# Both layers' rank rows in one result operand, results in the split x's memory, stores issued by ScalarE, SyncE's gathers spread around the x loads

## The reference

```python
def cond(x, A, B, ids):
    Bx = jnp.einsum('bni,bri->bnr', x, B[ids])
    return jnp.einsum('bnr,bor->bno', Bx, A[ids])
def L1_ffn(x, W, b, A, Bm, Wr):
    base_out = jnp.einsum('bsi,oi->bso', x, W) + b
    gates = softmax(jnp.einsum('bsi,ei->bse', x, Wr))
    proj_r = jnp.einsum('bsi,eri->bser', x, A)
    lora_out = jnp.einsum('bser,eor->bseo', proj_r, Bm)
    return base_out + jnp.einsum('bse,bseo->bso', gates * 2.0, lora_out)
x = x + L0_ffn(cond(x, L0_cond_A, L0_cond_B, itok_B_3_7), ...)
x = x + L1_ffn(cond(x, L1_cond_A, L1_cond_B, itok_B_4_50), ...)
```

## Time and profile before

| what | value |
|---|---|
| three runs, median (lowest to highest) | 353.43 us (350.32 to 354.69) |
| the profiled execution: its time / its span | 353.02 us / 351.0 us |
| TensorE matmuls busy | 326.0 us (93%), 2112 instructions |
| VectorE, ScalarE, GpSimd busy | 246.0 (70%), 149.8 (43%), 89.9 us (26%) |
| moved by DMA | 56.17 MB, mean 160 GB/s |

### The profile page before, as it was taken

One profiled execution on the slowest core, in us unless ns is written; L12 is line 12 of the kernel. 1 busy time (PEld: TensorE's weight loads), 2 busy tenths in 40 slices (PEclk: granted clock), 3 DMA queues, 4 the chain that ended last, 5 costly groups with the idle time before them and its releaser, 6 DMA issues.

```text
span 351.0 us, 6577 instructions
## 1 busy us (share of the span) xinstructions
PE 326.0 (93%) x2112; PEld 304.6 (87%) x2112; DVE 246.0 (70%) x496; ACT 149.8 (43%) x317; POOL 89.9 (26%) x61
## 2 busy tenths in 40 slices
PE   6998747889999999999999999999999999999975
PEld 5777647879999899989999999999999999999864
DVE  5925993797586867697668767775878586855554
ACT  5856833663065405550456036613562166203210
POOL 0014620184015500550046003620262026300000
PEclk9999898969999999999999999999999999999989
DMA  6889526611782078405950586048803780140005
GB/s 276 327 278 326 181 92 203 219 58 51 250 269 92 17 228 287 132 2 166 302 189 0 143 289 225 0 120 268 266 5 98 245 296 18 49 190 2 0 23 218
DMA packets 31525, 56.17 MB, mean 160 GB/s; under 512 B 3793, under 2 KB 21074, under 8 KB 31506
## 3 DMA queue, kind: packets, MB, share of 16 engines
q1 hardware_dynamic: 31506, 55.94, 47.9%
HBM read 39.15 MB, written 16.78 MB: 159 GB/s over the span
## 4 chain that ended last, share of the span: by engine, by line
PE 53%; issue 12%; DMA 10%; DVE 9%; POOL 6%; SPq 5%; ACT 4%; POOLq 0%; ACTq 0%; DVEq 0%
PE ps_d L316 12%; PE ps_d L318 12%; PE ps_d L317 12%; POOL xs_lo L917 5%; DMA xraw<-w 4%; DMA out<-xraw 3%; PE ps_h L323 3%; PE ps_p L316 2%; DVE k_lo L684 2%; PE ps_p L317 2%; PE ps_p L318 2%; PE ps_t L447 2%; DMA abraw<-ab_tab 2%; SPq L233 2%; SPq L235 2%
## 5 line engine op out<-in xcount | busy, mean ns | idle before, releaser
L917 POOL TENSOR_TENSOR xs_lo<-xraw,xs_hi 128x512 fp32r<-128x512 f32 x48 | 67.8, 1423 | 195.4 <-ACT xs_hi L520 195.3
L316 PE MATMUL ps_d<-w1s_hi,a1s_hi 128*128 128x384 f32 (+1 forms) x216 | 72.7, 337 | 1.8 <-DVE w1s_lo L684 1.8
L318 PE MATMUL ps_d<-w1s_hi,a1s_lo 128*128 128x384 f32 (+1 forms) x216 | 70.2, 325 | 0.0
L317 PE MATMUL ps_d<-w1s_lo,a1s_hi 128*128 128x384 f32 (+1 forms) x216 | 70.2, 325 | 0.0
L903 DVE SCALAR_TENSOR_TENSOR xraw<-ps_d,bsum,xraw 128x512 f32<-128x512 f32 x62 | 46.3, 750 | 27.5 <-PE ps_d L318 27.5
L520 ACT ACTIVATE xs_hi<-xraw 128x512 fp32r<-128x512 f32 x64 | 38.4, 624 | 17.6 <-DMA xraw<-x_in 11.1
L316 PEld LDWEIGHTS ps_d<-w1s_hi,a1s_hi 128*128 128x128 f32 x216 | 41.1, 190 | 3.9 <-DVE w1s_lo L684 3.8
L316 PE MATMUL ps_p<-xs_hi,bst_hi 128*128 128x256 f32 x128 | 39.4, 307 | 3.4 <-POOL xs_lo L917 2.5
L317 PEld LDWEIGHTS ps_d<-w1s_lo,a1s_hi 128*128 128x128 f32 x216 | 41.1, 190 | 0.0
L318 PEld LDWEIGHTS ps_d<-w1s_hi,a1s_lo 128*128 128x128 f32 x216 | 41.0, 190 | 0.0
L317 PE MATMUL ps_p<-xs_lo,bst_hi 128*128 128x256 f32 x128 | 37.8, 295 | 0.0
(11 more groups left out here) (156 smaller groups left out, 691.8 us busy)
## 6 DMA issues: line engine op xcount, KB each, us to landing
xraw<-x_in SPq DMA_DIRECT2D x32, 512.0 KB, 5.0
out<-xraw SPq DMA_DIRECT2D x32, 512.0 KB, 3.6
xraw<-w SPq DMA_DIRECT2D x16, 512.0 KB, 6.5
abraw<-ab_tab SPq DMA_DIRECT2D x64, 128.0 KB, 2.1
b0raw<-b_tab SPq DMA_DIRECT2D x64, 64.0 KB, 1.9
b0raw<-a SPq DMA_DIRECT2D x1, 512.0 KB, 3.7
lp<-exp SPq DMA_DIRECT2D x4, 69.0 KB, 7.5
cm<-exp_in SPq DMA_DIRECT2D x1, 144.0 KB, 5.3
```

The lines of the kernel that those rows point to most:

```text
L316: pe.matmul(acc, lh, rh, start=first, stop=False, skip_group_check=True)
L317: pe.matmul(acc, lh, rl, start=False, stop=False, skip_group_check=True)
L318: return pe.matmul(acc, ll, rh, start=False, stop=final, skip_group_check=True)
L917: return pool.tensor_tensor(dst, whole, high.bitcast(F32), ALU.subtract)
```

## The change

- **Result operand.** `res` [128, half, high/low, 1024] holds 64 rank rows of layer 1 and 64 rank rows of layer 0, the latter picked for the four sequences of a half. `from_layers(m)` takes it against the masked coefficients `cf` themselves (six matmuls of 256 columns). The experts' rows of both layers stand alone in `ew`, each twice in its 128 rows, against `ce`, whose rows hold the high and low parts of the coefficients: two matmuls of 512 columns.
- **Picking.** `m0` is stored to a DRAM table `m0_tab` ahead of the steps, and GpSimd fetches in each step the layer-0 rows of its eight sequences: `pick_m0`, eight DMAs of 16 rows x 2048 values (128 KB), after the last store of the step before has landed.
- **Expert part of the layer-1 coefficients.** `hle` x `ce`, two matmuls of 512 columns in place of six of 256; its splits have an instruction less.
- **Results** go to `done`, which lies over `xs` (the split x, used up by then), so that x loads wait for `d_out` only; ScalarE issues the stores at the end of its step; whoever writes `xs` again waits for `stored`.
- **SyncE's order.** Four sequences' gathers, x load 0, two sequences' gathers, x load 1, two sequences' gathers, x loads 2 and 3.
- **Start.** `hsb` and `lp` become one tile `misc`, which also receives layer 0's expert weights; it is zeroed after these are used (L773 of the changed kernel), and `init_done` moves to that memset. The experts' rows are loaded twice (ten small DMAs for five). In the last step, all five early result tiles start after `route(1)`.

```diff
+        xs_at = nc.sbuf_base
         xs = split("xs", [P, KT, HALF])
+
+        done_ = nc.alloc_sbuf_tensor_at("done", [P, KT * TOK], F32, offset=xs_at)
...
-        m1x = split("m1x", [P, 2, D])
+        res = sb("res", [P, 2, 2, D], F32R)
         k1 = split("k1", [P, TOK])
-        k2 = split("k2", [P, TOK])
-        c0s = split("c0s", [P, TOK])
+        cf = [sb(f"cf{i}", [P, 2, TOK], F32R) for i in range(2)]
+        ce = sb("ce", [P, TOK], F32R)
...
+                if k == 3:
+                    sp.wait_ge(m0_lo, len(WIDE_PARTS))
+                    sp.dma_start(m0_tab[:].rearrange("a r h n -> (a r) h n"), res[:, 0, :, :].bitcast(F32)
+                                 ).then_inc(m0_kept, 16)
                 if k == 6:
                     sp.wait_ge(w1_lo, 4)
-                    for e, n in enumerate(experts):
-                        r0 = E0ROWS[0].start + e * ER
-                        sp.dma_start(rows_raw[r0:r0 + ER, :],
-                                     exp0_rows[bass.ds(n, 1)].rearrange("a r o -> (a r) o")
-                                     ).then_inc(rows_in, 16)
-                    sp.dma_start(rows_raw[E1ROWS[0], :], exp1_rows).then_inc(rows_in, 16)
+                    for rows0, rows1 in (EHIGH, ELOW):
+                        for e, n in enumerate(experts):
+                            r0 = rows0.start + e * ER
+                            sp.dma_start(rows_raw[r0:r0 + ER, :],
+                                         exp0_rows[bass.ds(n, 1)].rearrange("a r o -> (a r) o")
+                                         ).then_inc(rows_in, 16)
+                        sp.dma_start(rows_raw[rows1, :], exp1_rows).then_inc(rows_in, 16)
...
-                    gather(picks, range(GROUP))
-                for i in range(CH):
-                    sp.wait_ge(d_out, KT * g + KC * (i + 1))
-                    sp.dma_start(out[bass.ds(g, 1), :, KC * i:KC * (i + 1), :]
-                                 .rearrange("a p k t -> p (a k) t"),
-                                 xraw[par][:, KC * i:KC * (i + 1), :]).then_inc(stored[i], 16)
-                    if ahead and i > 0:
-                        sp.wait_ge(stored[i - 1], 16 * g + 16)
-                        load_x(g + 2, par, i - 1)
-                if ahead:
-                    sp.wait_ge(stored[CH - 1], 16 * g + 16)
-                    load_x(g + 2, par, CH - 1)
+                    gather(picks, range(HSEQ))
+                    for i in range(CH):
+                        sp.wait_ge(d_out, KT * g + KC * (i + 1))
+                        load_x(g + 2, par, i)
+                        if i < 2:
+                            gather(picks, range(HSEQ + 2 * i, HSEQ + 2 * i + 2))
             steps(sp, body, 3)
...
-                product(ps_s[:], part(hts, ALL, ALL), part(k1, ALL, ALL), True, False)
-
-                pe.wait_ge(l_lo, 4 * g + 2)
-                for half in range(2):
-                    cols = slice(half * HALF, (half + 1) * HALF)
-                    mm = product(ps_s[:, cols], part(hls, ALL, half, ALL), part(k2, ALL, cols), False, True)
-                mm.then_inc(q_done, 1)
+                product(ps_s[:], hts, part(k1, ALL, ALL), True, False)
+
+                pe.wait_ge(l_lo, 2 * g + 1)
+                pe.matmul(ps_s[:], hle[:, 0, :], ce[:], start=False, stop=False, skip_group_check=True)
+                pe.matmul(ps_s[:], hle[:, 1, :], ce[:], start=False, stop=True, skip_group_check=True
+                          ).then_inc(q_done, 1)
...
-                def from_layer0(m):
-                    product(banks[m % len(banks)][:], part(m0s, ALL, slice(m * P, (m + 1) * P)), part(k1, ALL, ALL),
-                            True, False)
+                def from_layers(m):
+
+                    pe.wait_ge(m1_lo, 6 * g + (2 if m < 3 else 6))
+                    for half in range(2):
+                        cols = slice(half * HALF, (half + 1) * HALF)
+                        product(banks[m % len(banks)][:, cols],
+                                (res[:, half, 0, m * P:(m + 1) * P], res[:, half, 1, m * P:(m + 1) * P]),
+                                part(coefs, ALL, cols), half == 0, False)
...
-                    start_results((0, 1, 3))
+                    pe.wait_ge(m0_picked, 16 * GROUP * (g + 1))
                 else:
                     project(g + 1, 0)
                 pe.wait_ge(f1_lo, 2 * g + 2)
-                route(1, k2, f1s)
+                route(1, coefs, f1s)
+                pe.wait_ge(m0_picked, 16 * GROUP * (g + 1))
                 if last:
-                    start_results((4, 2))
+                    start_results((0, 1, 3, 4, 2))
...
-                        mm = product(banks[m % len(banks)][:, cols], part(m1x, ALL, half, slice(m * P, (m + 1) * P)),
-                                     part(k2, ALL, cols), False, True)
+                        from_layers(m)
+                    for w in (ew_hi, ew_lo):
+                        mm = pe.matmul(banks[m % len(banks)][:], w[:, m * P:(m + 1) * P], ce[:], start=False,
+                                       stop=w is ew_lo, skip_group_check=True)
...
+                    if half == 0:
+                        after_step(act, stored[i // KC], stored_by(g))
...
+                for i in range(CH):
+                    act.wait_ge(d_out, KT * g + KC * (i + 1))
+                    act.dma_start(out[bass.ds(g, 1), :, KC * i:KC * (i + 1), :]
+                                  .rearrange("a p k t -> p (a k t)"), done[i]).then_inc(stored[i], 16)
...
-            for t in (*hls, f1s, *k2):
+            for t in (hle, f1s, ce):
                 dve.memset(t[:].bitcast(F32), 0.0)
+            dve.memset(ew_lo[HR_:P, :].bitcast(F32), 0.0)
             dve.memset(hr[:, :, :, HC - 1:HC].bitcast(F32), 0.0)
-            dve.memset(hsb[:, 1, :], 0.0).then_inc(init_done, 1)
...
+            dve.tensor_copy(cb[:, 2, :], exp0_routerb).then_inc(small_lo, 1)
+            dve.wait_ge(small_lo, 3)
+            dve.memset(misc[:, P:], 0.0).then_inc(init_done, 1)
...
+                    if last and m % KC == 0:
+                        dve.wait_ge(stored[m // KC], 16 * g)
                     dve.wait_ge(d_done, KT * g + m + 1)
-                    dve.scalar_tensor_tensor(out=xraw[par][:, m, :], in0=banks[m % len(banks)][:],
+                    dve.scalar_tensor_tensor(out=done[m // KC][:, m % KC * TOK:(m % KC + 1) * TOK],
+                                             in0=banks[m % len(banks)][:],
...
+            def pick_m0(g):
+
+                layer0 = nc.values_load_multi_w_load_instructions(
+                    ids[0:1, bass.ds(g * GROUP, GROUP)], (mybir.EngineType.Pool,), min_val=0,
+                    max_val=ADAPT0 - 1)[1]
+                after_step(pool, d_done, KT * g)
+                after_step(pool, stored[CH - 1], 16 * g)
+                for b, n0 in enumerate(layer0):
+                    half = b // HSEQ
+                    r0 = L0ROWS[half].start + (b % HSEQ) * RANK
+                    pool.dma_start(res[r0:r0 + RANK, half, :, :],
+                                   m0_tab[bass.ds(n0, 1)].rearrange("a r h n -> (a r) h n")).then_inc(m0_picked, 16)
+
             split_x(0, 0, 0, range(CH))
             split_x(0, 0, 1, (0, 2))
             split_a(0)
+            pool.wait_ge(ids_in, 16)
+            pool.wait_ge(m0_kept, 16)
+            pick_m0(0)
             pool.wait_ge(w1_hi, POOL_CHUNK + 1)
             low(w1s[1][:, POOL_CHUNK, 0:D], w1raw[POOL_CHUNK], w1s[0][:, POOL_CHUNK, 0:D]).then_inc(w1_lo_pool, 1)
             def body(g, par, last):
+                if not (isinstance(g, int) and g == 0):
+                    pick_m0(g)
                 if not last:
```

139 lines of the change are left out of this document (69 added, 70 removed).

## The result

The changed kernel takes 399.1 us (median of 4 runs, 397.22 to 402.89) where the kernel before takes 353.4: a ratio of 1.132, 95% interval 1.121 to 1.143. It is 13% slower; 351 had been forecast, in a range that ends at 366. The profiled execution took 397.2 us, its span is 394.3.

A forecast was written before the change was run, and what follows sets the result against it. TensorE was taken to bound the steps, busy 35.89 of 36.20 us. 353.0 + 12.3 (start) - 1.5 - 2.1 - 1.0 (step 0) - 12.8 (steps) - 1.2 (last step) + 4.2 (waits) = 350.9, about 351; range 343 to 366.

The forecast's parts named there:

- the gathers, ahead of two x loads, at 5.5 to 7, I take 6.4: Loop steps: gathered rows land 6.4 us after the step's first ps_h matmul, so split_b ends at 8.6.
- rival 2: Loop steps: gathers queue against stores packet by packet, landing at about 8.6; 364 us or more; chance 0.13.
- 0.7 us a step: Loop steps: net new TensorE wait from late gathers and picks together, six times, +4.2 us.
- no slack: Before the transposes: today l_done at 216.67 meets turn() at 216.72; net wait put at 0 to 1.5 us a step.
- -8.6: Six loop steps: 12.8 us gained by fewer matmuls, 4.2 us lost to new waits.
- a step without waits: Loop steps: 34.1 us each, plus waits that name l_done or GpSimd's x split.
- +12.3 foreseen: Start: TensorE waits for the later init_done; from the projection on 12.3 to 12.6 us later, taken as +12.3.
- Nothing hides it: Start: the +12.3 us delay stays, since W1's chunks wait for buffers that the delayed matmuls free.
- -4.6 foreseen: Step 0: gains of 2.1 us from matmuls, 1.0 from a shorter split, 1.5 from GpSimd and VectorE parting.
- I took 0.9: GpSimd's picks: 0.9 us each, halfway between bounds of 0.515 and 1.27 us.
- Rival 1: Loop steps: GpSimd becomes the bound; at 1.27 us a pick TensorE waits 3.2 us a step, 366 us; chance 0.17.
- -1.2 foreseen: Last step: gain between 0.2 and 2.9 us from cheaper early tiles against idle TensorE, taken as 1.2.

The follow-up runs named there:

- e3: The changed kernel with SyncE issuing each store ahead of the x load, its order otherwise kept: 388.4 us, ratio to before 1.104.
- e2: The changed kernel with SyncE issuing all 16 gathers ahead of the four x loads again, ScalarE still issuing the stores: 373.3 us, ratio to before 1.059.
- e5: The kernel before with only SyncE's gathers spread around the x loads (eight, four, four): 385.0 us, before 351.8.
- e7: The kernel before with ScalarE issuing the stores at the end of its step, all 16 gathers ahead of the x loads: 352.4 us, ratio 1.002.
- e6: The kernel before with init_done raised behind the splits of W0 and the small weights: 364.9 us, ratio 1.041.
- e9: e4 with the picks of step 0 behind GpSimd's W1 chunk and the landing of the last W1 load: 366.1 us, ratio to before 1.038.
- e16: The changed kernel with the picks issued by SyncE behind its x loads, nothing else undone: 391.3 us, ratio to before 1.117.
- e14: e4 with the picks issued by SyncE a step earlier, as float32, behind the x loads: 345.8 us, before 351.4.
- e4: The changed kernel with init_done raised early again and all gathers ahead of the x loads: 366.0 us, ratio to before 1.038.

## Why the prediction was wrong, point by point

**The step that failed: "the gathers, ahead of two x loads, at 5.5 to 7, I take 6.4".** They landed at t = 9.8, later even than the 8.6 at which I had put the end of *all* transfers. Two things were wrong in this term. The first is the rank. I ranked the gathers by SyncE's program, ahead of two x loads and of the stores. In fact ScalarE's four stores are issued beside them (t = -5.2 to 1.5) and x loads 0 and 1 ahead of the last four, and the last gather lands 1.1 us after all of these (the last at 8.7). The second is the time of the DMA work: it ends later than 8.6, with x loads at 11.4 and, beside the picks, at 14.5. I took 271 and 403 GB/s for engines that are full; mixed, they moved 215 and 264 in the windows above. How the 3.4 us divide between the two no run shows. The rank is rival 2, to which I gave 0.13, with "SyncE issues two of the x loads behind them" against it: that doesn't protect gathers which are themselves issued late. The Trainium skill (DMA: Bandwidth & Descriptors, Queues, rings and completion order), which I cited there and set aside, has a DMA engine take turns between its queues packet by packet; the landing at 9.8, with stores of the other queue under way, agrees, though it doesn't single this rule out. In e3, with one queue, the wait at `turn()` falls from 29.9 to 6.5 us. In the changed kernel order and second queue act together: either undone (e2, e3) takes most of the wait at `turn()` away. On the kernel before, the order alone makes such waits (e5), and the second queue alone makes none (e7).

**The price of lateness.** I had 0.7 us a step. `split_b` ended at t = 12.0 instead of 8.6, and the transposes came 5.0 us later than before, as there was no slack behind it ("no slack", I had written, and then took the small end). The lower clock added 1.6 a step. Six steps: +26.9 instead of -8.6, an error of 35.5 us, three quarters of the miss. Even rival 2 was undersized, at 2.9 a step "more with the lower clock": the steps lost 6.7 each, from the 34.1 of a step without waits to 40.8.

**The start: +12.3 foreseen, +17.4 measured** at the first `ps_h` (62.01, before 44.57). The wait ends at 19.06 (foreseen 18.9). The dummies take 7.17 us instead of 6.15, and the transposes stand at 38.55 (foreseen 37.1): 14.8 later. The projection comes 14.2 later, and from there to `ps_h` it takes 15.5 us instead of 12.3, a stretch that I had taken as unchanged. TensorE waits 3.6 us in it for `xs_lo` (before: 1.8), and its granted clock over the stretch is 0.69 instead of 0.86. The mechanism was right, the size 5 us short. Alone on the kernel before (e6) it moves the first reduction by 15.4 us, gives 3.3 back in step 0, for which I had no term ("Nothing hides it"), and costs 13 us in the end.

**Step 0: -4.6 foreseen, +1.7 measured.** VectorE and GpSimd did part: `c0s_lo` took 0.69 us (foreseen 0.7), before 2.85. But what it gave was lost at the last W1 load, which needed 8.0 us instead of 4.3; while it was under way the DMA engines' share was 1.03 at 182 GB/s (before: 0.61 at 193). I had costed the picks of step 0 as time of GpSimd only. e9 shows that without the picks in front of it the W1 load is nearly in time, and e16 that this kernel gets 8 us back when they leave: its step 0 takes 44.2, 5.3 less than before. That is DMA time I did not price. That 5.3 is near my 4.6 is in part luck, since 3.3 of it comes with any late start (e6). The 1 MB store I had costed at nothing; no run takes it away, so its share stays open.

**The matmuls: right.** A tile takes 1.18 us (192.01 to 193.19). For a step without waits I had 34.1: e14 has one of 34.3, with TensorE busy for 34.0. VectorE's 0.75 us fits.

**The picks: cheaper than foreseen, and without effect here.** 4.41/8 = 0.55 us each, near my lower end of 0.515; I took 0.9. They started at t = 9.2 and not at 7. Rival 1 did not decide: with the picks off GpSimd (e16) the steps stay at 40 to 41, since the late gathers gave GpSimd its time. With these repaired (e4) it is the next bound: the true condition was where the picks start, not what one costs.

**The last step: -1.2 foreseen, -2.9 measured**, at the good end of the bounds (0.2 to 2.9).

The sum of errors: 5.4 (start), 6.3 (step 0), 35.5 (steps), -1.7 (last step): 45.5 of the 46.3 us between 350.9 and the profiled 397.2; the rest is 0.9 outside the span.
